# First cross attention: the key mask as a row of the keys' stacks instead of two matmuls per slot

## The reference

```python
qc = (xc @ cq_W).reshape(b, s, H, HD)
kc = (cond_tokens @ ck_W).reshape(b, LC, H, HD)
vc = (cond_tokens @ cv_W).reshape(b, LC, H, HD)
# _attn: s = q.k * scale; s = where(mask, s, finfo.min); softmax; @ v
cross = _attn(qc, kc, vc, cond_kv_mask[:, None, None, :]).reshape(b, s, d) @ co_W
x = x + g_x * cross
```

## Time and profile before

| | |
|---|---|
| median of 3 runs | 1338.84 us (1338.6 to 1342.22) |
| the profiled execution | 1344.21 us, of which the span of the trace is 1342.4 us |
| busy share of the span: PE, ACT, POOL, DVE | 89%, 66%, 67%, 55% |
| first cross attention, first and last mask matmul | 520.8 us and 834.4 us |

### The profile page before, as it was taken

The page is one execution under the profiler, slowest core; times in us unless marked ns, Lnnn a source line. Parts: engine busy times, 40 slices in busy tenths (PEclk is TensorE's granted clock), DMA queues, the critical chain, the costliest instruction groups (busy, mean ns, idle before and its releaser), DMA issues.

```text
span 1342.4 us, 42596 instructions
## 1 busy us (share of the span) xinstructions
PE 1196.5 (89%) x16674; PEld 664.3 (49%) x16674; DVE 736.5 (55%) x1613; ACT 888.5 (66%) x1527; POOL 900.0 (67%) x1798
## 2 busy tenths in 40 slices
PE   2455898899989888999999999899998999999998
PEld 2432454444444444555555555444443566666676
DVE  6213666667667665666666666222224566666553
ACT  0112565665666656778777777777876778888765
POOL 0018777777786866778778773466877778888742
PEclk9997999999999999999999999899999799999878
DMA  2425555455455444464565453000033456666651
GB/s 73 128 74 98 95 89 95 79 94 95 75 98 94 71 82 78 65 103 81 82 103 85 79 101 56 1 1 0 1 50 51 78 99 114 121 114 116 106 97 29
DMA packets 147257, 105.84 MB, mean 79 GB/s; under 512 B 25050, under 2 KB 146803, under 8 KB 147059
## 3 DMA queue, kind: packets, MB, share of 16 engines
q1 hardware_dynamic: 147058, 103.12, 43.1%
HBM read 9.08 MB, written 4.19 MB: 10 GB/s over the span
## 4 chain that ended last, share of the span: by engine, by line
PE 60%; POOL 15%; ACT 9%; issue 7%; SPq 1%; DVE 1%; DMA 0%; POOLq 0%; ACTq 0%
PE ps_po L580 10%; PE ps_st L559 6%; PE ps_nat L525 6%; PE ps_pj L477 5%; PE ps_pj L434 4%; PE ps_pj L460 4%; ACT p L824 4%; PE ps_pj L455 4%; PE ps_st L592 4%; PE ps_po L601 3%; PE ps_nat L533 3%; POOL ht L926 3%; PE ps_pj L468 2%; POOL ht L921 2%; PE ps_pj L440 2%
## 5 line engine op out<-in xcount | busy, mean ns | idle before, releaser
L660 DVE TENSOR_REDUCE negmax<-ps_nat 128x8 f32<-128x616 f32 (+1 forms) x384 | 360.9, 940 | 198.5 <-PE ps_nat L525 112.7
L824 ACT ACTIVATE p<-ps_st 128x1024 f32<-128x1024 f32 (+1 forms) x256 | 260.9, 1019 | 208.5 <-PE ps_st L559 206.5
L580 PE MATMUL ps_po<-p,vz 77*32 77x128 f32 (+1 forms) x6144 | 258.7, 288 | 2.6 <-ACT p L824 2.1
L882 POOL TENSOR_TENSOR ot<-vv,den 128x256 f32<-128x256 f32 x192 | 139.9, 729 | 150.3 <-ACT den L812 144.7
L824 ACT ACTIVATE p<-ps_st,key_bias 77x1024 f32<-77x1024 f32 x128 | 141.9, 1109 | 64.7 <-PE ps_st L559 64.7
L580 PEld LDWEIGHTS ps_po<-p,vz 77*32 77x32 f32 (+1 forms) x6144 | 150.5, 112 | 42.0 <-issue 6.4
L559 PE MATMUL ps_st<-stacks 64*77 64x128 bf16 (+1 forms) x3072 | 160.3, 226 | 7.3 <-ACT p L824 6.4
L525 PE MATMUL ps_nat<-stacks 64*128 64x77 bf16 (+1 forms) x3072 | 135.7, 211 | 3.6 <-DMA stacks<-parts 2.7
L525 PEld LDWEIGHTS ps_nat<-stacks 64*128 64x128 bf16 x3072 | 78.8, 97 | 116.3 <-issue 101.5
L894 POOL TENSOR_TENSOR whole<-whole,parts 128x512 f32<-128x512 f32 x96 | 98.9, 1030 | 51.3 <-ACT parts L759 51.1
L559 PEld LDWEIGHTS ps_st<-stacks 64*77 64x77 bf16 (+1 forms) x3072 | 106.6, 111 | 48.3 <-issue 26.5
(11 more groups left out here) (138 smaller groups left out, 2158.0 us busy)
## 6 DMA issues: line engine op xcount, KB each, us to landing
stacks<-parts SPq DMA_DIRECT2D x512, 128.0 KB, 3.1
stacks<-parts SPq DMA_DIRECT2D x256, 77.0 KB, 2.7
p<-in_x_dram SPq DMA_DIRECT2D x16, 256.0 KB
out_dram<-part SPq DMA_DIRECT2D x16, 256.0 KB, 2.3
stacks<-mt SPq DMA_DIRECT2D x192, 12.0 KB
p<-in_ctx_dram SPq DMA_DIRECT2D x16, 154.0 KB
stacks<-in_L_xcond_adaLN_W_dram SPq DMA_DIRECT2D x1, 576.0 KB
w<-in_L_xcond_mlp_W_dram SPq DMA_DIRECT2D x2, 256.0 KB
```

What stands on the lines that cost most here:

```text
L580: m = t.matmul(c.ps_po[step % 2][32 * g:32 * g + 32, S * p:S * p + S], c.vz[0:nk, i % 2, step % G, g, at:at + 32], c.p[0:nk, hh, S * g:S * ...
L660: v.tensor_reduce(c.negmax[:, step % 2, :].rearrange("p (h q g) -> p h q g", h=2, q=2)[:, :, p, :], c.nat_pair[:].rearrange("p (h n) -> p ...
L824: a.activation(c.p[0:nk, 2 * p:2 * p + 2, :].rearrange("p h n -> p (h n)"), c.st_pair[0:nk, :], ACT.Exp, bias=bias).then_inc(exped, 1)
L882: p.tensor_tensor(c.ot[:, i % 2, :, S * j:S * j + S], c.vv[:, step % 2, :].rearrange("q (p n) -> q p n", p=2), c.den[:, step % 2, :].rearr ...
```

## The change

The two mask matmuls are gone. The two spare rows of a stack get two purposes: one is for the maxima as before, the other for the key mask. On the queries' side the new row is one in the first feature's partitions (`first_d`), on the keys' side it holds the key mask. So the matmul of `natural` adds the mask itself. Since the same stacks serve `transposed`, where the mask comes in by `key_bias`, the queries' ones are overwritten with zeros before it.

```diff
             sp.wait_ge(rolled, 16 * 16)
+            sp.wait_ge(ready, 1)
+            for b in range(G):
+                for x in range(H // 2):
+                    sp.dma_start(c.key_sets[x:128:8, SC * b:SC * b + SC], c.key_rows[b:B:G, :]).then_inc(rolled, 16)
+            sp.wait_ge(rolled, 16 * 48)
...
-            v.memset(c.parts[:, 1], 1.0)
+            v.memset(c.parts[:, 1, 0:7], 0.0)
+            v.memset(c.parts[:, 1, 7:14], 1.0)
...
+            v.tensor_reduce(c.first_d[:], c.eye[:].rearrange("p (h e) -> p e h", e=HD)[:, 0], AX_X, ALU.add).then_inc(headed, 1)
+            dve.wait_ge(headed, 1)
+            v.tensor_copy(c.parts[:, 0, 6, :], c.first_d[:, 0:1].broadcast_to([128, NT]))
...
-                if i // NG == 1:
-                    for h in range(2):
-                        kept = c.ps_nat[h][:, 0:4 * nk].rearrange("p (g k) -> p g k", g=4)
-                        t.matmul(kept, c.eye_bf[:, step % B:step % B + 1].broadcast_to([128, S]),
-                                 c.key_rows[:].unsqueeze(1).broadcast_to([128, 4, nk]),
-                                 start=False, stop=True, skip_group_check=True).then_inc(nat_full, 1)
...
                 if p == 0:
-                    pe.wait_ge(max_here[step % 2], 16 * (step // 2 + 1))
+                    pe.wait_ge(max_here[step % 2], here(step))
...
+            def empty_keys():
+                for q in range(2):
+                    pool.wait_ge(stacked[1][q][(2 * NG - 1) % 3], 64 * ((2 * NG - 1) // 3 + 1))
+                p.memset(c.parts[:, 1, 6, :], 0.0).then_inc(emptied, 1)
...
-                sp.dma_start(qst[7 * (1 - i % 2):128:24, i % 3, :, S * j:S * j + S], c.mt[:, step % 2, :]).then_inc(max_here[step % 2], 16)
+                sp.dma_start(qst[7 - 6 * (i % 2):128:24, i % 3, :, S * j:S * j + S], c.mt[:, step % 2, :]).then_inc(max_here[step % 2], 16)
+                if i // NG == 1:
+                    sp.dma_start(qst[6 - 6 * (i % 2):128:64, i % 3, :, S * j:S * j + S], c.parts[0:16, 0, 7, 0:S]).then_inc(max_here[step % 2], 16)
+
+            def bring_keys(i):
+                g = i - NG
+                for p in range(2):
+                    sp.wait_ge(stacked[1][p][(i - 1) % 3], 64 * ((i - 1) // 3 + 1))
+                for p in range(2):
+                    sp.dma_start(c.parts[64 * p:64 * p + 64:8, 1, 6, 0:NC], c.key_sets[8 * g:8 * g + 8, :]).then_inc(keyed, 16)
...
+                if x == 1 and t == 0 and i // NG == 1:
+                    sp.wait_ge(keyed, 32 * (i - NG + 1))
...
+            key_slots = {slot_of(PER * i) - LEAD + 7: i for i in range(NG, 2 * NG)}
```

More of the change, by code:

```diff
@@ L50, in setup_phase @@
                                                  s("su_silu_d"), s("su_copied"))
+    headed = s("su_headed")
     made, masks, mask_ps, rolled = s("su_made"), s("su_masks"), s("su_mask_ps"), s("su_rolled")
@@ L93, in _ @@
                     sp.dma_start(c.rolled[r:r + 32, b, :], mask[32 * q:32 * q + 32, :]).then_inc(rolled, 16)
-            sp.wait_ge(rolled, 16 * 16)
+            sp.wait_ge(ready, 1)
[3 more added lines that the diff above has]
+            sp.wait_ge(rolled, 16 * 48)
         @block.gpsimd
@@ L381, in main_phase @@
     max_here = [s("max_here0"), s("max_here1")]
+    keyed, emptied = s("keyed"), s("emptied")
+    here = lambda step: 16 * (step // 2 + 1) + 16 * min(max(step // 2 + 1 - NG * G // 2, 0), NG * G // 2)
     st_full, exped, pv_done, values_kept = s("st_full"), s("exped"), s("pv_done"), s("values_kept")
@@ L527, in natural @@
                                      start=g == 0 and i >= NG, stop=g == 3, skip_group_check=True)
-                        if g == 3 and i // NG != 1:
+                        if g == 3:
                             m.then_inc(nat_full, 1)
-                if i // NG == 1:
-                    for h in range(2):
-                        kept = c.ps_nat[h][:, 0:4 * nk].rearrange("p (g k) -> p g k", g=4)
-                        t.matmul(kept, c.eye_bf[:, step % B:step % B + 1].broadcast_to([128, S]),
-                                 c.key_rows[:].unsqueeze(1).broadcast_to([128, 4, nk]),
-                                 start=False, stop=True, skip_group_check=True).then_inc(nat_full, 1)
             def turn_max(step):
@@ L666, in keep_max @@
                 if step >= 2:
-                    dve.wait_ge(max_here[step % 2], 16 * (step // 2))
+                    dve.wait_ge(max_here[step % 2], here(step - 2))
                 v.tensor_copy(c.mt[:, step % 2, :], c.turned_max[step % 2]).then_inc(max_kept, 1)
@@ L939, in _ @@
                     at_slot.setdefault(slot_of(PER * i) - LEAD + r, []).append((which, i, x))
+            def empty_keys():
+                for q in range(2):
+                    pool.wait_ge(stacked[1][q][(2 * NG - 1) % 3], 64 * ((2 * NG - 1) // 3 + 1))
+                p.memset(c.parts[:, 1, 6, :], 0.0).then_inc(emptied, 1)
             for slot in slots:
+                if slot == MLP_SLOT:
+                    empty_keys()
                 if even(unit_at(slot + 4)):
@@ L961, in bring_max @@
                 sp.wait_ge(max_kept, step + 1)
-                sp.dma_start(qst[7 * (1 - i % 2):128:24, i % 3, :, S * j:S * j + S], c.mt[:, step % 2, :]).then_inc(max_here[step % 2], 16)
+                sp.dma_start(qst[7 - 6 * (i % 2):128:24, i % 3, :, S * j:S * j + S], c.mt[:, step % 2, :]).then_inc(max_here[step % 2], 16)
[7 more added lines that the diff above has]
+                    sp.dma_start(c.parts[64 * p:64 * p + 64:8, 1, 6, 0:NC], c.key_sets[8 * g:8 * g + 8, :]).then_inc(keyed, 16)
             def bring_stack(i, x, t):
                 st, p = (qst, kst)[x], t // 4
+                if x == 1 and t == 0 and i // NG == 1:
+                    sp.wait_ge(keyed, 32 * (i - NG + 1))
+                if x == 1 and t == 0 and i == 2 * NG:
+                    sp.wait_ge(emptied, 1)
                 if t % 4 == 0:
@@ L989, in _ @@
                     bring_max(unit_at(slot + 3) // 2)
+                if slot in key_slots:
+                    bring_keys(key_slots[slot])
                 for i, x, t in at_slot.get(slot, []):
@@ L1025, in two_layers @@
         c.mask8 = sb("mask8", [S, S], U8)
-        c.key8 = sb("key8", [128, SC], U8)
         c.mask_nat = sb("mask_nat", [S, S], BF16)
@@ L1030, in two_layers @@
         c.key_bias = sb("key_bias", [128, B])
-        c.key_rows = sb("key_rows", [128, SC], BF16)
         c.eye = sb("eye", [128, 128])
@@ L1036, in two_layers @@
         c.eps = sb("eps", [128, 1])
+        c.first_d = sb("first_d", [128, 1])
+        c.key_sets = sb("key_sets", [128, NC], BF16)
         c.mod = sb("mod", [D, 13, B])
@@ L1064, in two_layers @@
         c.vec_rows = before[0:NVEC, 19 * D:20 * D]
+        c.key_rows = before[:, 20 * D:20 * D + 40].bitcast(BF16)[:, 0:SC]
+        c.key8 = before[:, 21 * D:21 * D + 20].bitcast(U8)[:, 0:SC]
         ps = lambda name, dt=F32: ctx.enter_context(nc.psum_tensor(name, [128, 512], dt))
```

## The result

The changed kernel takes 1357.55 us (median of 4 runs, 1356.62 to 1357.59) against 1338.72 us before (4 runs): 18.8 us slower, a ratio of 1.0138 with an interval of 1.0113 to 1.0162. The prediction said 1334 us, a range of 1314 to 1348 us and 27 in 100 for slower.

A forecast was written before the change was run, and what follows sets the result against it. TensorE bounds the first cross attention before, SyncE's queue after; gains of 15.4 + 7.4 + 2 = 24.8 us against setup's +20.2 give -4.6 us, 1339.6 profiled, 1334 us as median; range 1314 to 1348 us.

The forecast's parts named there:

- Setup, +20.2 us: End of setup: 32 added SBUF-to-SBUF DMAs on SyncE's queue at 0.63 us each, +20.2 us, none of it hidden.
- TensorE's saving, 0.37 us per unit: First cross attention: each removed mask matmul pair saves 0.37 us, 47.4 us for 128 pairs if TensorE stayed the bound.
- The queue becomes the bound: First cross attention: SyncE's work per group rises from 15.1 to 18.9 us, above TensorE's 17.3, so a group lasts 18.9.
- Gain: 14 x (20.0 - 18.9) = 15.4: First cross attention: about 14 groups with zeroing and stacks both queued last 18.9 us instead of 20.0, 15.4 us gained.
- the 2 us of head start: First cross attention: 2 us gained because SyncE's queue can lag somewhat before TensorE must wait for maxima.
- The last 20 slots: End of the first cross attention: no stacks left to bring, queue light, TensorE's full saving of 7.4 us.
- PE waits ahead of the transposed scores: First cross attention: maxima land late, so TensorE waits before the transposed scores of a step's first unit.
- the room of the maxima's landing: First cross attention: 4.4 us of queue lag are free before a late maximum makes TensorE wait.
- both hidden: SyncE's wait before bringing keys and the first k stack's wait for the keys cost nothing; otherwise tenths of a us per group.
- The rivals: Whole kernel: cheap issues (0.15), queue at the maxima's price (0.25), no saving on TensorE (0.05).
- The slower rival: First cross attention: zeroing at 0.83 us, SyncE 19.7 us a group, gain 12.6 us, whole +7.6 us, 1346 us; chance 0.25.
- The Trainium skill's sentence: Added DMAs cost next to nothing, gain 42.6 us; would lead to the cheap-issues rival, 1308 us, chance 0.15.

The follow-up runs named there:

- three_waits: Kernel before, with TensorE made to wait at three steps of the first cross attention for a maximum's landing, nothing added on any queue; 1360.42 us, ratio 1.0208.

## Why the prediction was wrong

- **Setup, +20.2 us:** right, +20.6 us, the issues at 0.589 us against 0.59 taken.
- **TensorE's saving, 0.37 us per unit:** right as work: 41 us less on the page. (ScalarE has 15.81 us in one of the twelve windows before, not 15.77 at most; nothing hangs on it.)
- **"The queue becomes the bound", a group 18.9 us:** right: 18.9 us is the mean of the periods without low clock. With the gaps behind them the four zeroing DMAs cost 0.64 us each (0.66 taken) and the two for the keys 1.3 us (1.2 taken).
- **What failed is the term that carries the 18.9 us through the stage, "Gain: 14 x (20.0 - 18.9) = 15.4", with the 2 us of head start.** It took a group with waits to be as long as SyncE's work in it. But TensorE, which had hardly waited in this stage before, now waits for landings, and the clock falls. The 14 groups took 273.2 us, 10.6 more than 14 x 18.9 - 2. In the stage the clock was 0.93 on average, and all that SyncE's queue took beyond 18.9 us a period lies in the periods with low clock. three_waits shows that a wait alone can do this.
- **The 20.0 of that term was too high as well.** Before, only the first eleven groups lasted 20.0 us; the next three took 19.1, 18.2 and 17.5 us, two of them less than 18.9 already. From the stage's first exponential to the first one of its fifteenth group (below, before and after) it is 274.9 us before, not 280, and 273.2 us after: a gain of 1.7 us for the 17.4 of the sum. 5.1 us of these 17.4 could be seen to be missing in the trace of before.

```profile
815.80 1.12 ACT L824 ACTIVATE p<-ps_st,key_bias 77x1024 f32<-77x1024 f32 x1
```

```profile
829.47 1.11 ACT L829 ACTIVATE p<-ps_st,key_bias 77x1024 f32<-77x1024 f32 x1
```

- **The last 20 slots, "PE's full saving comes: 20 x 0.37 = 7.4 us":** wrong. The last two groups took 32.7 us before and 32.5 us after. In these slots fewer projections stand between the units, so the slack in front of the stacks' and the maxima's landings is shortest. TensorE waits 2.13 us at 815 us for the group's last k stack, and the clock is at 0.66 in the window from 820 us.
- **"PE waits ahead of the transposed scores":** only in part. From 560 to 780 us it waited 7.5 us there for landings, and 11.4 us ahead of the natural scores, for a group's last k stack. The forecast worked out the room of the maxima's landing and had no term for that of the k stacks. (Its "both hidden" is about the waits for the keys' row; the changed kernel's profile shows neither from 560 to 780 us.)
- **The rivals.** The slower rival had the right sign for a wrong reason (the price of an issue, 0.83 us; it is 0.59). The Trainium skill's sentence, from "DMA: Bandwidth & Descriptors", section "Issuing engines are not separate DMA queues", that the issue is "usually small relative to the DMA itself" was rightly set aside: taking the zeroing off SyncE's queue alone brought 18.6 us. On the clock I used no row but those of the earlier trace rows, which could only tell that it is 1.00 while TensorE is never idle; none of the rivals had a clock that falls once TensorE waits. The trace of before had such rows in its other stages, as the self attention shows above.

What stays open: which waits bring the clock down and which don't, since waits of the same length did both; how long a low stretch then lasts; and how the 10.6 us divide exactly into late landings and clock, since a low stretch also gives the queue time to catch up.

## What to carry to other kernels

The issue of a DMA had a price on its queue that didn't go by what it moves: 0.59 us for 2.5 KB and for 9.9 KB. So before work is moved from the busiest engine to DMAs, sum the issues per period on the queue and place them where it waits; fewer and larger ones, another queue, or algebra that needs none of them (here: let the mask's row stay, and drop the bias) turned 18.8 us lost into 35.9 us gained. And an engine whose clock fell once it had to wait should not be priced by work alone: taking work away so that it begins to wait can cost more than the waits. Last, when a change touches one stage, compare that stage; the time of the whole carried some 9 us from a stage that did the same work.

## What the runs showed of the hardware

- Behind each of three waits of 3.3 to 3.9 us in full work TensorE's granted clock fell to 0.50 (1.2 GHz) and stayed there through windows in which TensorE was busy all the time; the groups that held them lasted 6.0 to 7.6 us longer. In the changed kernel 1.70 us of waiting, shortly after another of half a us, went ahead of such a stretch. Elsewhere waits of 1.68 and 2.11 us were followed by none.
- The same work of the second cross attention took 292.6 us at a mean clock of 0.91 and 283.3 us at 0.96.
- An issue of a DMA with both sides in SBUF took 585 to 597 ns for 64 rows (8 of them) and 501 to 592 ns for 16 rows (32 of them); ScalarE's queue issued the zeroing in 517 ns, SyncE's in 587 ns.
